# One vector read over two PSUM banks for the unmasked maxima of the attention scores

## The reference, cut to what matters

```
scores = jnp.einsum('bhqd,bhkd->bhqk', q, k) * scale          # 16 heads, 1024 x 1024, q and k have 48 rows
scores = jnp.where(causal[None, None], scores, jnp.float32(-jnp.inf))
attn = jax.nn.softmax(scores, axis=-1)
out = jnp.einsum('bhqk,bhkd->bhqd', attn, v)
```

## Time and profile before

| | |
|---|---|
| three runs | 2946.74, 2947.76, 2962.08 us (median 2947.76) |
| span of the profiled execution | 2947.5 us |
| TensorE busy | 2823.2 us, 96% |
| VectorE busy | 1869.7 us, 63% |
| ScalarE busy | 1806.7 us, 61% |
| L561, the reads without mask | 512, 329.1 us, 685 ns each |
| L418, the matmuls of the pairs | 1536 |

### The profile page before, as it was taken

The page is one execution under the profiler, slowest core; times in us unless marked ns, Lnnn a source line. Parts: engine busy times, 40 slices in busy tenths (PEclk is TensorE's granted clock), DMA queues, the critical chain, the costliest instruction groups (busy, mean ns, idle before and its releaser), DMA issues.

```text
span 2947.5 us, 51530 instructions
## 1 busy us (share of the span) xinstructions
PE 2823.2 (96%) x16460; PEld 1254.0 (43%) x16460; DVE 1869.7 (63%) x4636; ACT 1806.7 (61%) x2148; POOL 1243.5 (42%) x1325
## 2 busy tenths in 40 slices
PE   6789999999999999999999999999999999999999
PEld 2344444444444444444434444444444444444433
DVE  5665766756667566666666666675756657666553
ACT  1346675566755667456674576655766566655687
POOL 4311555126551364413644146531465225661254
PEclk9889999999999999999999999999999999999999
DMA  6303443034430444204432044321553124531243
GB/s 141 73 1 84 113 121 96 4 98 112 133 73 2 106 123 118 70 8 119 121 100 70 21 128 122 90 56 29 134 130 91 34 63 115 130 84 27 74 129 93
DMA packets 177556, 253.06 MB, mean 86 GB/s; under 512 B 51085, under 2 KB 83869, under 8 KB 177197
## 3 DMA queue, kind: packets, MB, share of 16 engines
q1 hardware_dynamic: 170300, 247.79, 32.9%
q10 hardware_dynamic: 6996, 1.99, 0.3%
HBM read 159.13 MB, written 12.63 MB: 58 GB/s over the span
## 4 chain that ended last, share of the span: by engine, by line
PE 85%; DVE 6%; issue 3%; ACT 2%; POOL 1%; SPq 0%; DMA 0%; ACTq 0%; DVEq 0%; POOLq 0%
PE ps L1236 17%; PE ps L1272 17%; PE ps L1290 16%; PE ps L1256 9%; PE ps L418 8%; PE ps L464 4%; PE ps L505 2%; PE ps L466 2%; PE ps L535 2%; DVE front L561 1%; PE ps L516 1%; DVE rest L1392 1%; PE ps L492 1%; PE ps L523 1%; PE ps L450 1%
## 5 line engine op out<-in xcount | busy, mean ns | idle before, releaser
L1356 ACT ACTIVATE rest<-ps 128x1024 f32<-128x1024 f32 x1024 | 993.7, 1024 | 341.2 <-PE ps L1272 341.1
L1338 ACT ACTIVATE rest<-ps 128x1024 f32<-128x1024 f32 (+3 forms) x768 | 608.6, 810 | 550.1 <-PE ps L1236 536.4
L1456 POOL TENSOR_TENSOR rest<-rest 128x512 f32<-128x512 f32 x478 | 631.9, 1322 | 560.6 <-DVE rest L1392 550.1
L1392 DVE SCALAR_TENSOR_TENSOR rest<-ps,b2c,wide 128x512 f32<-128x512 f32 x512 | 383.8, 750 | 490.4 <-PE ps L1290 460.7
L1272 PE MATMUL ps<-wide,w1s 98*128 98x512 f32 x2048 | 644.6, 434 | 11.5 <-ACT rest L1356 8.7
L1290 PE MATMUL ps<-rest,w2s 128*32 128x512 f32 x4096 | 546.1, 605 | 0.6 <-ACT rest L1356 0.6
L1446 POOL TENSOR_SCALAR_AFFINE_SELECT rest<-rest 128x256 f32<-128x256 f32 x512 | 204.3, 407 | 806.7 <-ACT rest L1338 803.6
L558 DVE CUSTOM_DVE_ANT_0 rest<-ps,maskd 128x256 f32<-128x256 f32 (+3 forms) x1024 | 458.7, 487 | 121.9 <-PE ps L418 114.6
L1236 PE MATMUL ps<-wide 49*128 49x512 f32 (+3 forms) x2304 | 485.7, 511 | 7.2 <-ACT rest L1338 6.1
L1272 PEld LDWEIGHTS ps<-wide,w1s 98*128 98x128 f32 x2048 | 346.0, 189 | 238.4 <-ACT rest L1356 109.4
L561 DVE TENSOR_REDUCE front<-ps 128x1 f32<-128x512 f32 x512 | 329.1, 685 | 103.7 <-PE ps L418 99.9
(11 more groups left out here) (138 smaller groups left out, 2225.0 us busy)
## 6 DMA issues: line engine op xcount, KB each, us to landing
wide<-gate_rows SPq DMA_DIRECT2D x1024, 128.0 KB, 2.8
wide<-front SPq DMA_DIRECT2D x480, 64.0 KB, 2.0
wide<-front SPq DMA_DIRECT2D x192, 128.0 KB, 2.4
ao<-in_x SPq DMA_DIRECT2D x16, 512.0 KB, 5.0
heads<-front SPq DMA_DIRECT2D x64, 128.0 KB, 2.4
xs<-in_x SPq DMA_DIRECT2D x16, 512.0 KB, 5.1
out<-xs SPq DMA_DIRECT2D x32, 256.0 KB, 2.7
wide<-ao SPq DMA_DIRECT2D x96, 64.0 KB, 2.3
```

Source lines behind the costliest of these rows:

```text
L1338: nc.scalar.activation(L.pt[:, u % PTS, :, f:HALF], L.ps[:, 2 * (u % 2):2 * (u % 2) + 2, 0:HALF - f], ACT.Exp, scale=SCALE).then_inc(S["c_ ...
L1356: nc.scalar.activation(L.hm[:, u % HM, :], bank(2 * (u % 2), 2), ACT.Gelu).then_inc(S["e_gelu"], 1)
L1392: v.scalar_tensor_tensor(out=dst, in0=bank(L2 + q % 2), scalar=L.b2c[:, e:e + 1], in1=L.gb[:, q // 2 % GB, q % 2, :], op0=ALU.add, op1=ALU ...
L1456: g.tensor_tensor(dst, dst, L.gy[:, k % GY, :], ALU.add).then_inc(S["e_add"], 1)
```

## The change

A pair without mask is looked up in the ring by the new method `side_by_side`. If its two places lie in two banks of which the second has the next number, VectorE waits once, for the second of the two matmuls, and one `tensor_reduce` reads both banks as a [128, 2, 512] operand and writes both maxima; it adds one to the count. `Ring.__init__` gives both places of such a pair that one count. All other pairs, and the masked ones, stay as they were. The order of the items, the banks and TensorE's instructions are unchanged, apart from the counts waited for.

```
         for item in items:
             e = READER.get(item[0], "v")
             self.start[item] = len(self.frees)
-            for _ in range(USES.get(item[0], 1)):
-                done[e] += 1
+            together = self.side_by_side(item)
+            for k in range(USES.get(item[0], 1)):
+                if not (together and k):
+                    done[e] += 1
                 self.frees.append((read[e], done[e]))
             self.end[item] = (read[e], done[e])
...
+    def side_by_side(self, item):
+
+        if item[0] != "pair" or item[3] == item[2] // 4:
+            return None
+        first, second = [self.banks[(self.start[item] + hh) % len(self.banks)] for hh in range(2)]
+        return first if second == first + 1 else None
...
     if kind == "pair":
         g, i, n, pr = item[1:]
         w = key_range(i, n).stop - n * HALF
+        first = R.side_by_side(item)
+        if first is not None:
+            v.wait_ge(S[R.filled], R.start[item] + 2)
+            m = pr * 4 + i % 4
+            v.tensor_reduce(L.mx1[:, g, m:m + 9:8, n], L.ps[:, first:first + 2, 0:w], AX.X, ALU.max).then_inc(read, 1)
+            return
         for hh in range(2):
```

## The result

| | before | changed |
|---|---|---|
| runs | 2946.74 to 2962.08 us (4) | 3023.50 to 3031.64 us (4) |
| median | 2949.20 us | 3029.70 us |
| ratio | | 1.0261, 95% interval 1.0242 to 1.0281 |
| profiled span | 2947.5 us | 3029.7 us |

The change makes the kernel slower by 2.6%, 77 us by the ratio and 82 us between the two profiled spans. I had forecast slower, 2998 us, with a range to 3020. The sign and the place were right, and the size was too small. The four runs of the kernel before lie 15 us apart. The longer runs of a kernel are those with the lower clock: of the 56 runs of the kernel before that stand beside the experiments, the shortest (2943.5 us) had a mean granted clock of 0.994 and the longest (2963.1 us) one of 0.983.

A forecast was written before the change was run, and what follows sets the result against it. TensorE was taken to bound the kernel, handing over with VectorE without backlog. To 2947.5 us the forecast added 41 us of stalls (2988.5) and 10 us of lower clock, giving 2998 us, range 2978 to 3020.

The forecast's parts named there:

- Where the change acts: Opening and attention stages: 127 of 256 unmasked pairs are joined, none in the expert stages; 254 reads become 127.
- The new read: VectorE's joined read of 1024 columns takes 1.22 us, bounds 1.11 and 1.37; the first bank is free 0.55 us later.
- The follower: TensorE's next matmuls needing a joined pair's first bank begin no sooner than 1.39 us after the read starts.
- The stalls: TensorE waits longer for first banks at 82 attention places: 42.3 us, less 1 us given back, +41 us.
- The part for the second matmul: The joined read must also wait for the pair's second matmul, taken as 0.02 us.
- The clock: Attention of images 1 to 7: 1.2 falls an image at 1.2 us each, 10 us; bounds none and 36 us.
- Rival 5: Attention stages: the clock falls three times an image or more, 3025 us; chance 0.10.
- Rival 1: Clustered reads on VectorE: each joined pair saves 0.07 us, the kernel gains 9 us, 2939 us; chance 0.02.
- Rival 2: Attention stages: later waits take up most of the stalls, 8 to 20 us remain, 2956 to 2968 us; chance 0.06.
- Rival 3: Whole kernel: nothing moves, as ring counts are met late anyway or few pairs are joined, 2948 us; chance 0.02.
- Rival 4: Attention stages: stalls as forecast but the granted clock stays where it is, 2983 to 2993 us; chance 0.25.

The follow-up runs named there:

- run 10: Kernel before with only the single wait: VectorE waits for the second matmul of 127 pairs, then two reads signal each on its own; 2959.1 us, ratio 1.0014.
- run 1: Changed kernel with the 127 pairs read by two one-bank instructions, only the second of which signals; 3021.7 us, ratio 1.0242.
- runs 5 and 6: Changed kernel joining, in attention, only 43 pairs whose follower comes late anyway: 2950.3 us; joining none in attention but 70 in expert stages, ring turned: 2952.2 us.
- run 6: Changed kernel with no pair joined in attention and the expert ring turned to banks 7, 6, so its 70 unmasked pairs are joined; 2952.2 us, ratio 0.9996.
- runs 5, 6 and 11: Runs 5 and 6, and both combined with an extra 256-column matmul at twelve places of image 0: 2945.6 us, ratio 0.9969.
- run 4: Changed kernel joining in attention only the early unmasked pairs, up to slot 23; 2996.0 us, ratio 1.0152.
- run 9: Changed kernel with an extra matmul of 4 columns at the 82 stalling places; 3024.0 us, ratio 1.0229.
- run 7: Changed kernel with an extra matmul of 128 columns at the 82 stalling places; 2995.3 us, ratio 1.0143.

## Why the prediction was right in kind and wrong in size

- **Where the change acts**: 127 joined reads and 258 single ones, as counted.
- **The new read**: 1.226 us in the attention stages and 1.216 in the expert stages; 1.22 was forecast from VectorE's own slope. ScalarE's slope (1.11) and two whole reads (1.37) were both off. (The bounds of 0.42 and 0.72 us would move the sum by -10.7 and +13.9 us over 82 places, a little more than the -10 and +13 that I wrote.)
- **The follower**: 1.38 us after the read's start, where 1.39 was forecast.
- **The stalls**: 4.7 us for a stage that kept its clock, where the forecast had 5.1 less 0.1. The eight full places gave 4.5 us (forecast 4.44). The place at 0.87 us gave 0.20 in place of 0.52, and the one at 1.27 us nothing in place of 0.12; what took up the rest there wasn't looked into. For the run that is some 39 us where the sum had 41. The part for the second matmul was taken as 0.02 us a place and is 0.05 (run 10).
- **The cause of the stalls**: the late release of the first bank (run 1), not the joined read itself (runs 5 and 6).
- **The clock** is the step that failed: "With one or two falls an image in the seven, say 1.2, that is 10 us", on falls of 3.4 us. The mechanism was right, and so nearly was the price, 1.2 us for 3.4 at the lower clock or 0.35 for one, measured 0.38. The amount of time at the lower clock was not. I had taken 1.2 x 3.4 x 7 = 29 us more at 1.2 GHz, and the attention stages had 134 in place of 25 us, 109 more. I took the shortest stretch of the earlier trace rows as the length of a fall; in image 3 one lasts 17.0 us and follows another after 3.5. The same rows spoke against it: a granted clock of 0.85 from 150 to 200 us is 15 us at 1.2 GHz in 50 (0.15 x 50 / 0.5). I had also left image 0 out of this term, though its clock was the one that already fell, and it had 27 us of the 109, up to 12 of which run 6 shows without the change. With 109 us at 0.38 in place of 29 at 0.35 the sum would have been 2988.5+41 = 3030, but both numbers are known only now, from the result itself. The upper bound of 36 us that stood beside the term (3 x 7 falls of 3.4 us, 71 us at 1.2 GHz) ends at 3025, below the measured time, and the range was cut at 3020, below that bound.
- **Rival 5** (2988.5+36, chance 0.10) was nearest. **Rival 1** is refuted by the result, and runs 5, 6 and 11 show no gain from VectorE's saved time. **Rival 2** is refuted as well: under 0.5 us an image was given back. **Rival 3** is refuted by the 127 joined reads and the result. **Rival 4**, stalls without the clock, is what image 1 and image 7 show, and not the other six. The instructions are the same in all of them, and which image falls differs from run to run (in run 1 it was 1 and 3 to 6, in run 4 images 2, 4, 6 and 7). Why one falls and the next does not wasn't tested.

The Trainium skill tells of a kernel that cycles through PSUM banks and whose clock goes up and down with short idle times between groups of matmuls (TensorE: Matmul & The Clock Gate, "A second HAM failure mode: psum-queue depth-cycling"). The trace after agrees, with 31.3 us lost in images 2 to 6, where no wait of TensorE was longer than 1.22 us; images 1 and 7 have waits as long (1.22 us) and no fall. The Trainium skill also advises, in Advanced Engine Details and Errata, "The Read-Write Bubble", to read several PSUM banks with one instruction: it does save time on VectorE, 7 us over the run, and nothing for the kernel.

## What to carry to other kernels

A signal belongs to a buffer, not to an instruction: before two buffers are released by one count, look in the timeline for consumers that start a fixed 0.14 us after the first release, for each of them pays nearly the whole second read, here 0.57 us of 0.69. Where new idle time stands between matmuls, price it twice, as waiting and as clock. For the clock, take the time at 1.2 GHz that a whole stage shows and not its shortest fall: image 0's attention had 24.9 us before, and those of images 1 to 7 had 0 to 23.9 after, 11.7 on average. If a wait can't be removed, work of no use in it can still pay: here an extra matmul of 128 or 256 columns in each long wait gave back 34 or 28 us of the 82 by the medians, and 0.3% on the kernel before.

## What the runs showed of the hardware

- One `tensor_reduce` of fp32 over two PSUM banks takes VectorE 1.216 to 1.226 us for 1024 columns. That is what 685 ns for the first 512 and the masked reads' slope of 1.04 ns a column give (1.22), so the step to the next bank shows no price.
- TensorE lost 0.38 us (result) and 0.40 us (run 9) for each us at 1.2 GHz in these stages and not 0.5. That waits which stood there in any case make the difference is likely and wasn't tested.
- The same instructions at the same stalls kept 2.4 GHz in image 1 and not in image 2, and which images fall differs from run to run.
- With an extra matmul of 128 columns in each of ten waits a stage, images 1 to 7 all stayed at 2.4 GHz (run 7); with one of 4 columns, five of the seven fell to 1.2 GHz (run 9).
